# K and V of all rows multiplied in a prologue and kept in DRAM, a router product with 16 columns, and a new order of steps, in a decoder layer on one core

## The reference, cut to what matters

```python
x = x + attn(layernorm(x))          # q, k, v by a short convolution and silu, rope, 4 heads, 64 slots,
                                    # a running softmax over time, gate, output projection
x = x + xattn(layernorm(x), ctx)    # 16 heads of 16, 77 context tokens, mask
x = x + ffn(layernorm(x))           # 8 experts of 64, the best 2 by router logits

# xattn
Q = queries @ W_q.T
K = ctx @ W_k.T                     # ctx: 32 x 77 x 256, needs nothing of x
V = ctx @ W_v.T
scores = where(mask, Q K^T / 4, -1e10); out = softmax(scores) V @ W_proj.T + b_proj
# ffn
logits = x @ gate_w                 # 256 -> 8
topv, topi = top_k(logits, 2); w = softmax(topv)
out = sum over the two of w * ((silu(x Wu[e]) * (x Wv[e])) Wo[e])
```

## Time and profile before

| | us |
|---|---|
| median of 3 runs | 1597.21 |
| lowest and highest | 1596.92, 1598.76 |
| the profiled execution's own time | 1600.0 |
| its span, first to last instruction | 1598.2 |

### The profile page before, as it was taken

The page is one execution under the profiler, slowest core; times in us unless marked ns, Lnnn a source line. Parts: engine busy times, 40 slices in busy tenths (PEclk is TensorE's granted clock), DMA queues, the critical chain, the costliest instruction groups (busy, mean ns, idle before and its releaser), DMA issues.

```text
span 1598.2 us, 32435 instructions
## 1 busy us (share of the span) xinstructions
PE 1517.5 (95%) x10912; PEld 1356.7 (85%) x10912; DVE 1221.1 (76%) x3060; ACT 986.8 (62%) x2671; POOL 825.6 (52%) x937
## 2 busy tenths in 40 slices
PE   3599999999999999999999999999999999999986
PEld 3478888998888989888898989889888988988864
DVE  3767788878778887877888787788887778888643
ACT  2466666666666666666666666666666666666641
POOL 3354655555465555556554555655465565546320
PEclk9989999999999999999999999999999999999987
DMA  5000000000000000000000000000000000000000
GB/s 144 1 12 13 19 19 18 18 10 13 19 19 19 18 17 7 17 19 19 19 18 16 7 18 19 19 19 18 16 6 19 19 19 19 18 16 6 10 9 14
DMA packets 88819, 29.56 MB, mean 18 GB/s; under 512 B 68304, under 2 KB 88656, under 8 KB 88656
## 3 DMA queue, kind: packets, MB, share of 16 engines
q1 hardware_dynamic: 88656, 27.49, 7.4%
HBM read 16.55 MB, written 8.39 MB: 16 GB/s over the span
## 4 chain that ended last, share of the span: by engine, by line
PE 68%; DVE 11%; issue 9%; POOL 8%; ACT 3%; SPq 0%; DMA 0%; POOLq 0%; ACTq 0%; DVEq 0%
PE bank L389 56%; DVE a_conv L818 8%; PE bank L395 6%; PE bank L623 3%; POOL a_Er_lo L1392 2%; POOL a_qkr L1399 2%; POOL a_o L1430 2%; DVE x_nmax L943 1%; ACT a_Er_hi L1165 1%; PE bank L702 1%; PE bank L477 1%; ACT x_prob L1264 0%; DVE a_rC L840 0%; SPq L379 0%; ACT x_Q_stack L1251 0%
## 5 line engine op out<-in xcount | busy, mean ns | idle before, releaser
L1264 ACT ACTIVATE x_prob<-bank,x_nmax 128x77 f32<-128x77 f32 x1024 | 249.0, 331 | 144.0 <-DVE x_nmax L943 143.8
L943 DVE TENSOR_REDUCE x_nmax<-bank 128x4 f32<-128x308 f32 x256 | 121.2, 474 | 132.0 <-PE bank L389 129.2
L389 PE MATMUL bank<-x_Vbd,x_probT 128*128 128x34 f32 (+1 forms) x1280 | 164.9, 265 | 0.2 <-ACT x_probT L1275 0.2
L389 PEld LDWEIGHTS bank<-x_Vbd,x_probT 128*128 128x128 f32 x1280 | 163.0, 193 | 0.3 <-ACT x_probT L1275 0.3
L818 DVE SCALAR_TENSOR_TENSOR a_conv<-a_raw,cw,a_conv 128x256 f32<-128x256 f32 x384 | 154.9, 478 | 9.3 <-POOL a_conv L1387 9.3
L1275 ACT ACTIVATE x_probT<-bank 128x256 f32<-128x256 f32 (+1 forms) x256 | 112.8, 441 | 70.6 <-PE bank L623 70.6
L1392 POOL TENSOR_TENSOR a_Er_lo<-a_E,a_Er_hi 128x512 fp32r<-128x512 f32 x32 | 41.5, 1296 | 178.4 <-ACT a_Er_hi L1165 178.4
L623 PE MATMUL bank<-ident,x_prob 128*128 128x128 f32 x640 | 115.1, 278 | 1.5 <-ACT x_probT L1275 1.5
L840 DVE RECIPROCAL a_rC<-bank 128x512 f32<-128x512 f32 x32 | 107.1, 3346 | 3.4 <-PE bank L389 3.4
L389 PE MATMUL bank<-x_K_bd,x_Q_stack 128*128 128x308 f32 x256 | 92.7, 362 | 7.6 <-ACT x_prob L1264 6.0
L843 DVE TENSOR_TENSOR a_AT<-bank,tri 128x512 f32<-128x512 f32 x128 | 87.1, 681 | 14.0 <-PE bank L389 13.0
(11 more groups left out here) (254 smaller groups left out, 5537.1 us busy)
## 6 DMA issues: line engine op xcount, KB each, us to landing
x<-in_x SPq DMA_DIRECT2D x32, 256.0 KB, 2.7
out<-x SPq DMA_DIRECT2D x32, 256.0 KB, 2.1
ctxT<-in_ctxT SPq DMA_DIRECT2D x32, 77.0 KB, 2.0
x_Vbd<-x_Vtok SPq DMA_DIRECT2D x128, 9.6 KB
keep<-in_mask SPq DMA_DIRECT2D x32, 19.2 KB, 2.0
f_s<-in_fWu SPq DMA_DIRECT2D x2, 256.0 KB, 5.7
x_Vbd<-x_Vtok SPq DMA_DIRECT2D x32, 6.0 KB
x_Vbd<-x_Vtok SPq DMA_DIRECT2D x32, 3.6 KB
```

Of the source, the lines that this page charges most:

```text
L389: return pe.matmul(out, lhsT, rhs, start=start, stop=stop, skip_group_check=True)
L943: dve.tensor_reduce(nmax[:, u % 2, :], X0[:, 0:UH * S2].rearrange("p (h s) -> p h s", h=UH), AX.X, ALU.min).then_inc(on.x_max, 1)
L1264: ins = act.activation(prob[:, col:col + S2], X0[:, i * S2:(i + 1) * S2], ACT.Exp, scale=-1.0, bias=nmax[:, u % 2, i:i + 1])
```

## The change

- **K and V.** `x_k`, `x_v`, `x_kl` and the per-row context loads are gone. The context comes as one array of 256 x 2560 (32 rows of 77 tokens side by side, padded), cut into 5 groups of 512 columns, and is loaded at the start into tiles that are free then. A new step `g_mm` makes, for each group, two pieces of K and two of V; pieces 0 to 7 stand in pass 0, 8 to 15 in pass 1, 16 to 19 in pass 2, all in the N phase of PE's list. ACT copies them out (`g_out`), DVE makes K's low half (`g_lo`), SP stores them to DRAM (`g_store`: `k_hi`, `k_lo`, `v_tok`). Later each row's K is read from there by three DMAs (`x_kin`) and V by twelve (`x_vbd`, now from DRAM).
- **Router.** The two halves of the router weights stand side by side as 16 columns, so `f_gate` has four products (16 columns of weights) instead of six; `f_lg` is two transposes; `f_logit` adds the two halves of the logits instead of copying.
- **Order.** All five `body` lists are new. The pass now begins with `A(a_vtok)`: `a_vtok`, `a_ktok`, `a_A` and `a_state` moved from phase N at the end of a pass to phase A at the start of the next, and `x_proj` is the last step.

The diff, cut to its core:

```diff
+CTX, GW = 2560, 512
+NG, GT = CTX // GW, GW // P
...
-        fgate = halves("fgate", [P, KC, NE])
+        fgate2 = sb("fgate2", [P, KC, 2, NE], F32R)
+        fgate = [fgate2[:, :, i, :] for i in range(2)]
...
+        homes = [flat_p[:, 0:GW], flat_p[:, GW:2 * GW]] + [t[:].rearrange("p c d -> p (c d)") for t in (
+            x1[0], x1[1], xn["x"], xn["f"])] + [fth[:]] + [t[:] for t in g_ctx]
+        ctx_in = [homes[KC * g:KC * (g + 1)] for g in range(NG)]
...
+            def g_store(r, m):
+                n = 4 * r + m
+                if n >= 2 * NG:
+                    return
+                g = n // 2
+                if n % 2 == 0:
+                    sp.wait_ge(on.g_hi, 2 * (g + 1))
+                    sp.wait_ge(on.g_lo, 2 * (g + 1))
+                    for half, dst in zip(k_out, (a["k_hi"], a["k_lo"])):
+                        sp.dma_start(dst.rearrange("(j p) s -> p j s", p=P)[:, :, g * GW:(g + 1) * GW],
+                                     half.rearrange("p (j s) -> p j s", j=KC).bitcast(F32)).then_inc(kv_out, 16)
...
+            def x_kin(r):
+                written(r)
+                if r > 1:
+                    sp.wait_ge(on.x_kbd, upto(r - 2))
...
-                L(a_load); F(f_store); L(x_load); A(x_vbd)
+                N(g_store, 0); N(g_store, 1); N(x_load); N(g_store, 2); N(g_store, 3); L(a_load); A(x_vbd)
+                F(f_store); N(x_kin)
...
+            def g_mm(r, m):
+                n = 8 * r + m
+                if n >= 4 * NG:
+                    return
+                g, i = divmod(n, 4)
+                dst = G_BANK[i]
...
+                if i < 2:
+                    ins = features(dst[:, :], lambda k: xwk[:, k, i * P:(i + 1) * P], lambda k: ctx_in[g][k])
+                else:
+                    for t in range(2):
+                        at = ((i - 2) * 2 + t) * P
+                        ins = features(dst[:, t * D:(t + 1) * D], lambda k: ctx_in[g][k][:, at:at + P],
+                                       lambda k: xwv[:, k, :])
+                ins.then_inc(on.g_ps, 1)
...
-                mm_halves(F1[0:NE, 0:T], [
-                    (lambda i, k=k: fgate[i][:, k, :], lambda i, k=k: xnT["f"][i][:, k, :]) for k in range(KC)
-                ]).then_inc(on.f_gate_ps, 1)
+                for k in range(KC):
+                    for i in range(2):
+                        ins = mm(F1[0:2 * NE, 0:T], fgate2[:, k].rearrange("p i e -> p (i e)"), xnT["f"][i][:, k, :],
+                                 start=(k == 0 and i == 0), stop=(k == KC - 1 and i == 1))
...
-                    ins = mm(F1[:, T + c * NE:T + (c + 1) * NE], lgT[:, c * P:(c + 1) * P], ident[0:NE, 0:NE])
+                    ins = pe.transpose(F1[:, T + c * 2 * NE:T + (c + 1) * 2 * NE], lgT[:, c * P:(c + 1) * P],
+                                       ident[0:2 * NE, 0:2 * NE])
...
-                X(x_pt, 7); X(x_av, 6); F(f_st, 1); X(x_av, 7); N(a_et); A(a_wo); X(x_ot); F(f_yy); N(a_vtok)
-                N(a_A, 0); X(x_proj); A(x_k); N(a_ktok); A(x_v); A(x_turn); N(a_A, 1); N(a_state)
+                A(a_vtok); N(g_mm, 0); N(g_mm, 1); A(a_ktok); A(a_A, 0); X(x_turn); A(a_A, 1); A(a_state)
+                N(g_mm, 2); N(a_turn); X(x_q); F(f_turn); A(a_ok); N(a_qk); X(x_s, 0); F(f_gate); F(f_u0)
...
```

More of the change, by code:

```diff
@@ L222, in build @@
         ld_c = [sem(f"ld_c{i}") for i in range(2)]
+        ld_g = [sem(f"ld_g{i}") for i in range(2)]
+        kv_out = sem("kv_out")
+        k_in = [sem(f"k_in{i}") for i in range(2)]
+        vbd_in = [sem(f"vbd_in{i}") for i in range(2)]
         st_y = [sem(f"st_y{i}") for i in range(2)]
-        vbd_in = sem("vbd_in")
         w_ready = sem("w_ready")
@@ L566, in x_turn @@
                 turn(X0, xn["x"]).then_inc(on.xnT_ps["x"], 1)
[L568 to L586, removed]
+            def g_mm(r, m):
[4 more added lines that the diff above has]
+                dst = G_BANK[i]
+                if g > 0:
+                    if i < 2:
+                        pe.wait_ge(on.g_lo, 2 * (g - 1) + i + 1)
+                        pe.wait_ge(on.g_hi, 2 * (g - 1) + i + 1)
+                    else:
+                        pe.wait_ge(on.g_v, 2 * (g - 1) + i - 1)
+                if n == 0:
+                    pe.wait_ge(ld_g[0], 16 * (2 + KC))
+                if g == 1 and i == 0:
+                    pe.wait_ge(ld_g[1], 16 * KC * (NG - 1))
+                if i < 2:
+                    ins = features(dst[:, :], lambda k: xwk[:, k, i * P:(i + 1) * P], lambda k: ctx_in[g][k])
+                else:
+                    for t in range(2):
[3 more added lines that the diff above has]
+                ins.then_inc(on.g_ps, 1)
             def x_q(r):
@@ L729, in F @@
                         f(rf, *k)
[L732 to L735, removed]
-                X(x_s, 7); X(x_pt, 4); N(a_c); X(x_pt, 5); X(x_av, 4); A(a_ot); X(x_pt, 6); X(x_av, 5)
-                X(x_pt, 7); X(x_av, 6); F(f_st, 1); X(x_av, 7); N(a_et); A(a_wo); X(x_ot); F(f_yy); N(a_vtok)
-                N(a_A, 0); X(x_proj); A(x_k); N(a_ktok); A(x_v); A(x_turn); N(a_A, 1); N(a_state)
+                A(a_vtok); N(g_mm, 0); N(g_mm, 1); A(a_ktok); A(a_A, 0); X(x_turn); A(a_A, 1); A(a_state)
+                N(g_mm, 2); N(a_turn); X(x_q); F(f_turn); A(a_ok); N(a_qk); X(x_s, 0); F(f_gate); F(f_u0)
+                N(g_mm, 3); X(x_pt, 0); X(x_s, 1); F(f_lg); N(a_v); A(a_qt); X(x_s, 2); F(f_v0); N(a_s)
+                X(x_s, 3); A(a_P, 0); A(a_P, 1); X(x_pt, 1); X(x_av, 0); X(x_s, 4); X(x_pt, 2); A(a_o)
+                X(x_av, 1); X(x_pt, 3); F(f_st, 0); X(x_s, 5); N(g_mm, 4); N(a_g); F(f_u1); X(x_pt, 4)
+                X(x_av, 2); X(x_s, 6); F(f_v1); X(x_pt, 5); X(x_av, 3); N(g_mm, 5); X(x_s, 7); N(g_mm, 6)
+                N(a_c); X(x_pt, 6); A(a_ot); N(g_mm, 7); X(x_av, 4); F(f_st, 1); X(x_pt, 7); X(x_av, 5)
+                X(x_av, 6); X(x_av, 7); N(a_et); A(a_wo); X(x_ot); F(f_yy); X(x_proj)
             def others():
@@ L1273, in x_pt @@
                     act.wait_ge(on.x_av_ps, upto(r - 1, NU, QU + u + 1))
+                if r == 0 and u == 0:
+                    act.wait_ge(kv_out, KV_OUT * NG)
                 g = GROUPS[u % QU]
@@ L1560 @@
            for n, v in arrays.items()}
+    for n, shape in (("k_hi", (D, CTX)), ("k_lo", (D, CTX)), ("v_tok", (CTX, D))):
+        aps[n] = nc.dram_tensor(n, shape, F32).ap()
     aps["out"] = nc.dram_tensor("out_0", (B, T, D), F32, kind="ExternalOutput").ap()
```

169 lines of the change are left out of this document (100 added, 69 removed).

## The result

The changed kernel takes 1518.72 us (median of 4 runs, 1517.06 to 1518.82), the kernel before 1597.07 us beside it: a ratio of 0.9508, 95% interval 0.9491 to 0.9524.

A forecast was written before the change was run, and what follows sets the result against it. TensorE's executed work was taken to bound the steady periods. 29 periods losing 2.12 us each (-61.5), prologue +10 and drain -2.5 make -54 us: 1546, and with the median 2.8 us lower 1543 us, range 1529 to 1568.

The forecast's parts named there:

- Work removed from a period: TensorE, each period: K 0.84, V 0.87, two router products 0.24, turning the logits 0.27; sum 2.22 us less.
- The wait of +0.1 us with the bound of -0.26: New period: 0.1 us of wait for reciprocal and x load together; bounds -0.26 (today's idle time goes) and +0.8 us.
- In this stretch the time is what TensorE executes.: The 29 steady periods: TensorE busy for 1346.37 of 1353.80 us, idling 0.26 us a period, so its work sets the time.
- a product removed from the periods pays in full: Steady periods: each TensorE product taken out shortens the period by its whole time.
- Steps of the order: New period laid end to end: tight at reciprocal `a_rC` (under 1 us) and x load; K and V DMAs cost nothing.
- The margin of the load: Next x lands at 43.2 us of the new period, `a_stats` could start at 43.6: 0.4 us to spare.
- Fill: Before the steady periods: prologue pieces +2, +6 and +5, less 3.4 for K and V: about +10 us, bounds 0 and 31.
- Drain: After the steady periods: row 31's K and V and the router's saving, partly inside waits: -2.5 us.
- Rival, the x load late: Load of next x fully late, seen at `a_state`: 0.8 us x 29 = 23 us, 1566 us; chance 0.15.
- Rival, VectorE's chain: Run from `a_conv` to `a_rC` on VectorE becomes the bound: period 47.2 us, +22, 1619 us; chance 0.08.
- Rival, small DRAM reads: K's and V's fifteen DMAs take 30 us, TensorE waits 6 us before `x_av 0`: 1717 us; chance 0.03.
- Rival, the prologue not hidden: The K and V pieces at the start cost 31 us instead of 10: 1564 us; chance 0.12.

The follow-up runs named there:

- Experiments 1 and 3: experiment 1, and the kernel before with only the 16-column router weights, two transposes of the logits and the adding `f_logit`: 1589.12 us, ratio 0.9951.
- experiment 1: The changed kernel with the lists of before for TensorE, VectorE, ScalarE and GpSimd, SyncE's list staying new: 1588.71 us, ratio 0.9951.
- experiment 4: The changed kernel with each of the 20 prologue pieces replaced by one short bf16 product, so K and V are left out: 1515.26 us, ratio 0.9489.
- experiment 10: The changed kernel with SP's `f_store` ahead of `a_load`, so the next x is loaded later: 1670.38 us, ratio 1.0441.
- experiment 6: The changed kernel with VectorE's list alone in the order of before: 1719.20 us, ratio 1.0743.
- the square: Four runs with the new router: order of before with K and V per period 1589.1 us, in the prologue 1588.7; new order 1570.5 (prologue as well) and 1518.7.
- The halves: The changed kernel with all four lists cut at one point, one half in the order of before: first half new 1587.05 us, second half new 1576.72 us.
- experiment 8: The changed kernel with all four lists cut behind `a_v` on TensorE, first half new, second half in the order of before: 1587.05 us, ratio 0.9922.

## Why the prediction was right in direction and wrong in size

- *Work removed from a period.* Right: 2.22 us forecast; K and V 1.71, the router's products 0.25 and its turns 0.31 by start distances in the changed kernel, 2.27.
- *The wait of +0.1 us with the bound of -0.26.* This term failed. The period lost 2.91 us, 0.64 more than the work: times 29 the difference to the forecast's 2.12 is 22.9 of the 27.6 us by which the span was missed. The bound took TensorE's 0.26 us of idle time for all of its waiting. Busy time does not show the part of a wait that the tail of a matmul covers (0.28 us long, 0.12 apart): in the kernel before, the product after `x_negmask` at 839.27 starts 0.41 us later, with 0.14 the pace of such a product; its row has no mark of a wait. In the changed kernel the next product (845.51, after 845.47) follows at once. Experiments 1 and 3 show the same from the other side, 0.50 of 1.71 and 0.31 of 0.56 us cashed in.
- *"In this stretch the time is what TensorE executes."* The sentence behind the failed bound. The chain of before spends 13.16 us of each period off TensorE and 33.54 on it, so the period was that of this loop and not TensorE's work of 46.04 us. All the removed products lay in the loop's part on TensorE, and yet the removed 2.27 us bring only 0.81 in the order of before (46.68 to 45.87, experiment 1), since new waits, for `x_out` and `x_Q_stack`, come into the same chain. That "a product removed from the periods pays in full" was true only because the order changed with it. The prediction laid out the new order to look for new waits, and never laid out the old one, where it would have found the waits to be removed. The chain's 68% said so.
- *Steps of the order.* Right in outcome: no waits for the reciprocal, K, V or the load. The margin of the load was met (0.4 us), that of the reciprocal was forecast at some 0.8 us and is 0.26.
- *Fill.* +6.0 against +10. The pieces ahead of row 0 brought `a_qk` to the full pace, and `a_c` of row 1 lost its wait of 4.94 us: the stretch of granted clock 0.81 is 1.00 now. The Trainium skill (TensorE: Matmul & The Clock Gate, section "Part 1: The HAM clock gate (the "warmup" mystery)") has activity release the clock. The row-0 pace and experiment 4 agree: 0.11 us a product with full pieces ahead and 0.21 with small ones, granted clock 0.98 and 0.86. The sum held that effect in part only.
- *Drain.* -3.1 against -2.5, right.
- *Rival, the x load late.* It did not occur, but its price was far off: 0.8 us forecast for a load fully late; in experiment 10 VectorE waits 3.4 us for it on average (108.4 us in 32 rows, by the page), and a period is 5.4 us longer. It named `a_state` as the waiter; `x_out` stands in the same queue, and `x_turn` waits for it first. It also left out the clock, on average 2.0 of the 5.4 us.
- *Rival, VectorE's chain.* Did not occur in the new order, but experiment 6 shows how near it is: one list out of step costs 200 us, about a third of it by the clock.
- *Rival, small DRAM reads.* Did not occur. V's pieces are issued in 0.81 us each from DRAM (median of 384) against 0.84 from SBUF in the kernel before, and `x_av 0` never waits for them. The Trainium skill (DMA: Bandwidth & Descriptors, section "Why small descriptors are slow (HBM only)") speaks of their bandwidth; here some 14 us of room hide it, and the row shows no dearer issue.
- *Rival, the prologue not hidden.* No: some 3.5 us, within the noise, for 30 us of products in the new order. In the old order it would have come close, +16 us of fill.

Of the 78 us, then: the router in the old order brings 8.0 (1597.1 to 1589.1), the prologue with it 0.4 (1588.7), and the new order on top 70.0 (1518.7). In another sequence the shares are others; that is what the square shows.

What stays open: which single placements hold the old order up. The halves were cut at one point only, and no run changes one step and gains.

## What to carry to other kernels

TensorE at 95% busy and 68% of the chain was two bounds close together here, its own work (46.04 us) and a loop through other engines (46.68). Before counting removed work in full, lay out the present order too, and ask which wait ends last once the work is gone. In a software pipeline written as one list for each engine, an order is a property of all the lists; a single list taken over from another order was worse than either whole order (1719 and 1841 against 1519 and 1589 us). Price TensorE's waits with the clock that they lose.

## What the runs showed that was not expected

- A wait of 4.94 us cost 7.8 us of the period (experiment 10), as the granted clock fell to 0.50 behind it. It takes less than that: with waits of 2.33 us and below, 4.6 us in all, 28 of 29 periods had a stretch at the lower level (experiment 6), and with none above 1.07 us ten of 29 (experiment 8). Waits of some 0.7 us (experiment 1) left it at 1.00.
- In the fill, 30 us more of products cost 3.5 us at most by the medians, and in the profiled executions `x_q` of row 1 started at 139.25 us with full pieces and at 141.78 with small ones.
- The sensitivity: VectorE's order alone, with the same instructions, is worth 13% of the time (1719.2 against 1518.7 us), the lower clock that follows its waits included.
